# Fetching a third of the far degree factors from HBM and moving the message product to ScalarE in a three-layer graph kernel

## The chip, the cores and the metric

The kernel runs on one core of a Trainium2 chip. The metric is the device time of one execution in microseconds (us). The profile is one execution recorded by the hardware profiler. Engines are named as in the profile: PE is TensorE, PEld its weight loads, DVE VectorE, ACT ScalarE, POOL GpSimd. SP is the engine that issues most DMAs; "SPq" in a row is such an issue.

## The reference

A graph with 100,000 nodes of 64 features and 25,000 edges. Layer 0 is an attention layer; after it come three rounds ("layers" below, l = 0, 1, 2) of the code that matters here. Each round computes one mask value per edge, sums it per source node, and weighs far rows with it:

```python
for l in range(N_LAYERS):
    f1 = relu(x[row] @ nb_W[l] + nb_b[l])
    f2 = relu(x[col] @ self_W[l] + self_b[l])
    h = relu(concatenate([f1, f2], axis=1) @ att1_W[l] + att1_b[l])
    log_alpha = (h @ att2_W[l] + att2_b[l])[:, 0]
    mask = clip(sigmoid(log_alpha) * (ZETA - GAMMA) + GAMMA, 0.0, 1.0)
    rowsum = segment_sum(mask, row, num_segments=n) + 1e-06
    d_inv_sqrt = clip(rowsum ** (-0.5), 0.0, 10.0)
    vals = mask * d_inv_sqrt[row] * d_inv_sqrt[col]
    x = segment_sum(vals[:, None] * x[col], row, num_segments=n)
    out = out + x
```

`d_inv_sqrt[col]` is the degree factor of the edge's other end, the "far" one. In the program `x[col]` is called `far`, and `mask * d_inv_sqrt[row]` is `VAL0`.

## The kernel before

The edges stand sorted by their own node, in 196 tiles of 128 edges, four tiles to a chunk, 49 chunks (`NC1`). Each layer l has a mask stage (five matmul steps per chunk, with gathers of far rows on POOL from l = 1 on), a short degree part (`rowsum_dve`), and then the **sum stage**, which the change edits. Every engine runs its own list of steps. `staged(n, [(lag, step), ...])` writes such a list: in iteration i it emits each step for chunk i - lag, in the order given. An engine works its list strictly in that order and stops at a semaphore wait, so a step that waits also holds everything behind it. The steps of a sum stage for chunk c are:

- **spread** (SP): a DMA that broadcasts the bf16 row numbers of the chunk's far factors, `row_d`, over 128 partitions into `RB` (names `XC<-row_of_far_degree` in the trace). `RB` has two buffers.
- **hot** (ACT): two operations, Square into `OFF` and Relu into `OH`, that make a one-hot matrix of 128 x 512.
- **bring** (PE): 12 matmuls of the one-hot matrix with the table `TAB` of degree factors (three bf16 parts); two sets of banks.
- **select** (DVE): four operations that pick one column each into `DCc`, then a small product with `VAL0` into `VAL1` (signal `o_val`), and then the **product** of the far rows with `VAL1` into `Z`, 128 x 256 (signal `z_done`).
- **turn_z** (PE): two transposes of `Z`. **scan** (DVE): the segment sum over the turned rows. **turn_back** (PE): two transposes of the sums.
- In layers 0 and 1: **rows** (ACT) copies the turned sums from PSUM into `TS` (signal `q_out`), and **store** (SP) waits for `q_out` and writes them to HBM. When all are stored, POOL gathers the far rows of the next layer.
- In layer 2: **load** (SP) brings base rows and the sums of both earlier layers, three DMAs; for chunk c it waits until **final** (DVE, three additions, signal `q2_fin`) is through with chunk c - 3, whose buffer it takes. POOL then scatters the final rows to `out`, four indirect DMAs per chunk.

The lags before are: SP spread 0, store 5 (layer 2: load 2); ACT hot 0, rows 4; PE bring 0, turn_z 2, turn_back 3; DVE select 0, scan 2, final 3. So SP's order is spread(i), store(i-5), spread(i+1), and ACT's is hot(i), rows(i-4), hot(i+1). On POOL a memset of the far rows of layer 0 follows each product.

## Time and profile before

| | |
|---|---|
| median of 3 runs | 3198.88 us (3198.11 to 3206.03) |
| the profiled execution, its own time | 3199.13 us |
| span of its trace | 3197.3 us |
| sum stage of layer 0, about | 2003 to 2164 us |
| sum stage of layer 1, about | 2456 to 2618 us |
| sum stage of layer 2, to the end | 2912 to 3197 us |
| busy over the span | DVE 69%, POOL 60%, PE 56%, ACT 33% |
| mean granted clock of PE | 0.687 of full speed |

The times inside the trace count from the start of its span. A row of the timeline gives start, duration, engine, line, operation, and in brackets how long the engine had been idle and what ended that. Line numbers are those of the kernel before. Two operations in a row on DVE or ACT overlap by about a tenth of a microsecond, so the distance from start to start is shorter than the duration.

### The profile page before, as it was taken

To read this page: it belongs to the slowest core of one execution; us is meant where nothing else is said; L and a number is where in the kernel's file an instruction comes from. 1 tells how busy PE (TensorE), PEld (TensorE's weight loads), DVE (VectorE), ACT (ScalarE), POOL (GpSimd) and SP (SyncE) were. 2 spreads that over 40 slices of the span, in tenths; PEclk is the share of its full clock that TensorE was granted. 3 is DMA by queue.
4 is the path that set the end of the run, shared out by engine and by line. 5 is a ranking of instruction groups with operands and counts; after the bars stand their busy time and mean duration, and the time that the engine had idled before them with its cause. 6 is when DMAs were issued, how large, how long until landed. Compare 5 with 4: busy or idle time off the path is not lost.

```text
span 3197.3 us, 34323 instructions
## 1 busy us (share of the span) xinstructions
PE 1780.0 (56%) x8972; PEld 1443.3 (45%) x8972; DVE 2195.2 (69%) x5951; ACT 1068.3 (33%) x2292; POOL 1913.7 (60%) x1844
## 2 busy tenths in 40 slices
PE   1124444441399986653665654665665656655663
PEld 0023333331299975542454433453444544544442
DVE  6748888887877744434555553897866988766775
ACT  0024444442144420001333323553444644443221
POOL 0057777777888017776777775017773017773776
PEclk9975555565555555556777776897888987787555
DMA  0023332231122212214222211233332333333543
GB/s 7 3 54 82 84 88 82 83 86 41 41 86 86 83 60 69 71 50 96 62 63 61 64 40 34 70 85 96 98 104 64 88 88 94 102 98 84 126 119 85
DMA packets 283933, 238.03 MB, mean 74 GB/s; under 512 B 161125, under 2 KB 207611, under 8 KB 283637
## 3 DMA queue, kind: packets, MB, share of 16 engines
q1 hardware_dynamic: 226933, 196.13, 21.4%
q0 software_dynamic: 56832, 40.05, 5.5%
q8 instruction: 58, 0.95, 0.1%
q14 instruction: 110, 0.90, 0.1%
HBM read 163.62 MB, written 84.20 MB: 78 GB/s over the span
## 4 chain that ended last, share of the span: by engine, by line
POOL 48%; issue 18%; DVE 13%; PE 12%; DVEq 4%; DMA 2%; SPq 1%; ACT 1%; POOLq 0%; ACTq 0%
POOL big L1003 13%; POOL G L994 12%; POOL regs L1845 7%; POOL out L1010 6%; POOL regs L1854 5%; PE bank L923 5%; POOL x_after_layer L647 5%; DVE den L1271 3%; PE bank L916 3%; DVE big L1285 2%; DVE big L1591 2%; PE bank L872 1%; DVEq L1590 1%; PE bank L1451 1%; DVEq L1273 1%
## 5 line engine op out<-in xcount | busy, mean ns | idle before, releaser
L1003 POOL DMA_INDIRECT big<-layer_rows,late x392 | 425.9, 1087 | 305.8 <-SPq L1075 186.9
L1845 POOL DMA_INDIRECT regs<-in_x,G x200 | 213.8, 1069 | 234.8 <-DVEq L1711 174.1
L1451 PE MATMUL bank<-regs,SQ 99*128 99x256 bf16 x1764 | 274.8, 319 | 84.2 <-ACT SQ L1357 77.7
L647 POOL DMA_INDIRECT x_after_layer<-G,idx_s x200 | 197.0, 985 | 198.0 <-DVEq L808 135.9
L1870 POOL DMA_INDIRECT farf<-dst_float,VAL x196 | 252.8, 1290 | 59.7 <-issue 59.7
L1451 PEld LDWEIGHTS bank<-regs,SQ 99*128 99x128 bf16 x1764 | 189.3, 112 | 152.8 <-ACT SQ L1357 102.7
L1010 POOL DMA_INDIRECT out<-G,scat_i x196 | 194.7, 993 | 104.4 <-issue 61.4
L1854 POOL DMA_INDIRECT regs<-in_x,G x200 | 211.2, 1056 | 70.2 <-issue 59.7
L1271 DVE SCALAR_TENSOR_TENSOR den<-steps,late,bank 128x256 f32<-128x256 f32 x588 | 245.2, 472 | 9.6 <-PE bank L1451 9.3
L994 POOL DMA_INDIRECT G<-x_after_layer,own_i x196 | 200.6, 1023 | 69.2 <-issue 61.0
L994 POOL DMA_INDIRECT G<-x_after_layer,far_i x196 | 198.5, 1013 | 66.5 <-issue 66.5
L505 PE MATMUL bank<-regs 128*128 128x196 bf16 x800 | 161.2, 356 | 90.8 <-ACT regs L492 90.8
L1355 ACT ACTIVATE SQ<-XC,row_of 128x512 bf16<-128x512 bf16 x147 | 105.9, 721 | 259.4 <-DMA XC<-row_of_far_degree 235.6
L1402 PE MATMUL bank<-ident,big 128*128 128x128 f32 x196 | 50.3, 347 | 226.8 <-DMA big<-layer_rows,late 226.8
L1398 PE MATMUL bank<-ident,XC 128*128 128x128 f32 x196 | 50.3, 408 | 215.2 <-DVEq L1114 215.2
L564 ACT ACTIVATE SQ<-XC 128x512 f32<-128x512 f32 x99 | 62.3, 629 | 284.8 <-DVE XC L547 284.7
L395 DVE RECIPROCAL dstat<-dstat 128x8 f32<-128x8 f32 (+1 forms) x196 | 38.9, 198 | 169.8 <-ACT dstat L408 169.8
L885 PE MATMUL bank<-ident,VS 128*128 128x128 f32 x100 | 32.6, 426 | 212.5 <-DVE VS L717 212.5
L933 PE MATMUL bank<-big,den 128*128 (+1 forms) x400 | 95.8, 420 | 93.4 <-DVE den L587 86.5
L1402 PEld LDWEIGHTS bank<-ident,big 128*128 128x128 f32 x196 | 23.2, 166 | 271.1 <-issue 270.9
L933 PEld LDWEIGHTS bank<-big,den 128*128 128x128 f32 x400 | 87.3, 322 | 106.7 <-issue 99.4
L1398 PEld LDWEIGHTS bank<-ident,XC 128*128 128x128 f32 x196 | 33.0, 206 | 226.0 <-issue 226.0
(416 smaller groups left out, 5745.7 us busy)
## 6 DMA issues: line engine op xcount, KB each, us to landing
regs<-x_after_layer SPq DMA_DIRECT2D x96, 256.0 KB, 3.2
out<-regs SPq DMA_DIRECT2D x96, 256.0 KB, 2.1
XC<-row_of_far_degree SPq DMA_DIRECT2D x147, 128.0 KB, 3.4
den<-in_x SPq DMA_DIRECT2D x50, 256.0 KB, 2.7
x_after_layer<-den SPq DMA_DIRECT2D x50, 256.0 KB, 2.0
regs<-tile_nodes SPq DMA_DIRECT2D x50, 256.0 KB, 3.2
layer_rows<-TS SPq DMA_DIRECT2D x98, 128.0 KB, 2.0
regs<-in_x SPq DMA_DIRECT2D x46, 256.0 KB, 2.8
```

What stands on the lines that cost most here:

```text
L505: pe.matmul(o_, GE[b][h][:, k * P:(k + 1) * P], LT[:, h, part, :], start=(h + part == 0), stop=False)
L647: g.indirect_dma_start(x1_d, bass.IndirectOffsetOnAxis(ap=idx_s[:, b, k:k + 1], axis=0), G[:, b, k, 0, :], None, bounds_check=top, oob_is_ ...
L923: ins = pe.matmul(bank[4 + b][:, k * F:(k + 1) * F], ZTs[b][:, q * 512 + k * P:q * 512 + (k + 1) * P], wm[:, q, :], start=(q == 0), stop=( ...
L933: ins = pe.matmul(bank[b][:, k * F:(k + 1) * F], STg[b][:, k, :], big1[:, one(c, k), :].rearrange("p o f -> p (o f)"), start=True, stop=True)
L994: g.indirect_dma_start(G[:, b, grp // 2, grp % 2, :], None, x1_d, bass.IndirectOffsetOnAxis(ap=ix[:, u:u + 1], axis=0), bounds_check=top, ...
L1003: ahead(g, l, REVERSED, lambda u, l=l: g.indirect_dma_start(far[:, tile_of(u // C, u % C), :], None, xt_d[l - 1], bass.IndirectOffsetOnAxi ...
L1010: g.indirect_dma_start(out, bass.IndirectOffsetOnAxis(ap=scat_i[1][:, u:u + 1], axis=0), SUM[b][:, k, :], None, bounds_check=top, oob_is_e ...
L1271: v.scalar_tensor_tensor(PICK[k], steps[:, :], far_c[:, u:u + 1], bank[2 + 2 * b + k // 2][:, (k % 2) * 256:(k % 2) * 256 + 256], ALU.is_e ...
L1451: ins = pe.matmul(bank[2 + 2 * b + k // 2][:, (k % 2) * 256:(k % 2) * 256 + 256], OH[b][0:RB1 + 1, k * P:(k + 1) * P], TAB[0:RB1 + 1, part ...
L1845: g.indirect_dma_start(GR[:, c % DEEP, k, 0, :], None, a["x"], bass.IndirectOffsetOnAxis(ap=own0[:, c * C + k:c * C + k + 1], axis=0), bou ...
L1854: g.indirect_dma_start(GR[:, c % DEEP, k, 1, :], None, a["x"], bass.IndirectOffsetOnAxis(ap=far0[:, c * C + k:c * C + k + 1], axis=0), bou ...
L1870: g.indirect_dma_start(farf[:, u:u + 1], None, dstf_d, bass.IndirectOffsetOnAxis(ap=perm1[:, u:u + 1], axis=0), bounds_check=top, oob_is_e ...
```

## The change

Three things are done together.

1. In layers 0 and 1 the chunks 5, 8, 11, ..., 47 (15 of 49) are `FETCHED`: SP writes the degree factors as a table to HBM once per layer (`table_out`), and POOL gathers each fetched chunk's 512 factors from it with four indirect DMAs (`fetch_degrees`). These chunks have no spread, no hot, no bring and no picks. The other 34 are `LOOKED` and are numbered through by `g`, which picks their buffers. Layer 2 has all 49 looked up as before.
2. In all three layers the product moves from DVE to ACT, as four operations of 128 x 64 with a scale of one value per partition. It stands in ACT's list at lag 1, between hot and rows.
3. The lags behind it grow by one: scan 3, turn_back 4, rows 5, final 4. The lags of SP's list stay: store 5, load 2.

```diff
+FETCHED = [[c for c in range(NC1) if l < 2 and c >= 5 and c % 3 == 2] for l in range(3)]
+LOOKED = [[c for c in range(NC1) if c not in FETCHED[l]] for l in range(3)]
+LOOKED_BEFORE = [sum(len(LOOKED[k]) for k in range(l)) for l in range(4)]
...
+            def fetch_degrees(l):
+                g.wait_ge(signal("tables_out"), 16 + 32 * (l + 1))
+                for c in FETCHED[l]:
+                    i = fetch_index(l, c)
+                    landed = signal(f"pair{i % FARS}")
+                    if i >= FARS:
+                        g.wait_ge(landed, fetch_need(i - FARS))
+                    for u in range(C * c, C * c + C):
+                        g.indirect_dma_start(DCc[:, u:u + 1], None, deg_d, bass.IndirectOffsetOnAxis(ap=pos_i[:, u:u + 1], axis=0),
+                                             bounds_check=places, oob_is_err=False).then_inc(landed, 16)
...
+                def table_out(l=l):
+                    sp.wait_ge(signal("r_val"), l + 1)
+                    for h in range(2):
+                        sp.dma_start(at(deg_d, 256 * h, [[512, 49], [1, 256]]), DEGR[49 * h:49 * h + 49, :]).then_inc(signal("tables_out"), 16)
...
-                    staged(NC1, [(0, spread), (5, store)])
+                    staged(NC1, [(0, spread), (1, lambda c: table_out() if c == 0 else None), (5, store)])
...
             def select(c):
                 b = c % 2
...
+                if c in FETCHED[l]:
+                    i = fetch_index(l, c)
+                    v.wait_ge(signal(f"pair{i % FARS}"), fetch_need(i))
+                else:
...
                 v.tensor_tensor(VAL1[:, C * c:C * c + C], DCc[:, C * c:C * c + C], VAL0[:, C * c:C * c + C], ALU.mult).then_inc(signal("o_val"), 1)
-                if c >= 2:
-                    v.wait_ge(signal("z_t"), l * NC1 + c - 1)
-                v.drain()
-                v.tensor_tensor(by_pair(Z[b]), by_pair(far[:, C * c:C * c + C, :]), bc(VAL1[:, C * c:C * c + C].rearrange("p (h q) -> p q h", h=2), F), ALU.mult).then_inc(signal("z_done"), 1)
...
-            staged(NC1, [(0, select), (2, scan)] + ([(3, final)] if l == 2 else []))
+            staged(NC1, [(0, select), (3, scan)] + ([(4, final)] if l == 2 else []))
...
-                staged(NC1, [(0, hot)] + ([(4, rows)] if l < 2 else []))
+
+                def product(c, l=l):
+                    b = c % 2
+                    s_.wait_ge(signal("o_val"), l * NC1 + c + 1)
+                    if c >= 2:
+                        s_.wait_ge(signal("z_t"), l * NC1 + c - 1)
+                    for k in range(C):
+                        u = C * c + 2 * (k % 2) + k // 2
+                        ins = s_.activation(Z[b][:, k, :], far[:, C * c + k, :], ACT.Copy, scale=VAL1[:, u:u + 1])
+                    ins.then_inc(signal("z_done"), 1)
+                staged(NC1, [(0, hot), (1, product)] + ([(5, rows)] if l < 2 else []))
...
-                staged(NC1, [(0, bring), (2, turn_z), (3, turn_back)])
+                staged(NC1, [(0, bring), (2, turn_z), (4, turn_back)])
```

On SP, in the sum stage of layer 0, the list begins like this before (`XC<-row_of_far_degree` is a spread, `layer_rows0<-TS` a store):

```order
L1058 DMA XC<-row_of_far_degree 128x512 [waits h_cc,h_t,row_out]
L1058 DMA XC<-row_of_far_degree 128x512
L1058 DMA XC<-row_of_far_degree 128x512 [waits o_hot] x4
L1062 DMA layer_rows0<-TS 128x4x64 [waits q_out]
L1058 DMA XC<-row_of_far_degree 128x512 [waits o_hot]
L1062 DMA layer_rows0<-TS 128x4x64 [waits q_out]
```

and like this after:

```order
L1093 DMA XC<-row_of_far_degree 128x512 [waits h_cc,h_t,row_out]
L1093 DMA XC<-row_of_far_degree 128x512
L1084 DMA degree_of_place<-den 49x256 [waits r_val]
L1084 DMA degree_of_place<-den 49x256
L1093 DMA XC<-row_of_far_degree 128x512 [waits o_hot] x3
L1097 DMA layer_rows0<-TS 128x4x64 [waits q_out]
L1093 DMA XC<-row_of_far_degree 128x512 [waits o_hot]
L1097 DMA layer_rows0<-TS 128x4x64 [waits q_out]
L1093 DMA XC<-row_of_far_degree 128x512 [waits o_hot]
L1097 DMA layer_rows0<-TS 128x4x64 [waits q_out] x2
```

Store(i-5) still stands between spread(i) and spread(i+1); of each three spreads one is gone, its store is not, and the table goes out behind the second spread.

On ACT, in the same stage, from the hot of chunk 5 on before (L1355 and L1357 are hot, L1348 is rows):

```order
L1355 ACTIVATE SQ<-XC,row_of 128x512 [waits o_mm,o_ids1]
L1357 ACTIVATE SQ<-SQ,one_c 128x512
L1348 ACTIVATE TS<-bank7 128x2x2x64 [waits s_bt]
L1355 ACTIVATE SQ<-XC,row_of 128x512 [waits o_mm,o_ids0]
L1357 ACTIVATE SQ<-SQ,one_c 128x512
L1348 ACTIVATE TS<-bank6 128x2x2x64 [waits q_stored0,s_bt]
```

and after, from the product of chunk 4 on (L1394 and L1396 are hot, L1405 the product, L1384 is rows; `bank6` and `bank7` take turns with the chunk, so the first rows(0) is the one with `bank6`):

```order
L1405 ACTIVATE den<-big,VAL1 128x64 [waits z_t,o_val]
L1405 ACTIVATE den<-big,VAL1 128x64 x3
L1384 ACTIVATE TS<-bank6 128x2x2x64 [waits s_bt]
L1394 ACTIVATE SQ<-XC,row_of 128x512 [waits o_mm,o_ids1]
L1396 ACTIVATE SQ<-SQ,one_c 128x512
L1405 ACTIVATE den<-big,VAL1 128x64 [waits z_t,o_val]
L1405 ACTIVATE den<-big,VAL1 128x64 x3
L1384 ACTIVATE TS<-bank7 128x2x2x64 [waits s_bt]
L1394 ACTIVATE SQ<-XC,row_of 128x512 [waits o_mm,o_ids0]
```

Before, the rows of chunk 1 (`bank7`) follow the hot of chunk 5; now they follow the hot and the product of the next iteration, that of chunks 6 and 5. The rows of chunk i-5 stood ahead of hot(i) and now stand behind it.

On DVE, where the sum stage of layer 2 comes to its first final, before (L1285 is scan, L1271 and L1274 are select, L1278 is the product, L1295 to L1301 are final; `bank4` and `bank5` belong to odd chunks, `bank2` and `bank3` to even ones):

```order
L1285 SCALAR_TENSOR_TENSOR big<-regs,bank0 128x256 [waits z_t]
L1271 SCALAR_TENSOR_TENSOR den,late<-steps,late,bank4 128x256 [waits o_mm]
L1271 SCALAR_TENSOR_TENSOR den,late<-steps,late,bank4 128x256
L1271 SCALAR_TENSOR_TENSOR den,late<-steps,late,bank5 128x256 x2
L1274 TENSOR_TENSOR VAL1<-late,VAL0 128x4
L1278 TENSOR_TENSOR den<-big,VAL1 128x256 [waits z_t]
L1285 SCALAR_TENSOR_TENSOR big<-regs,big,bank1 128x256 [waits z_t,s_scan]
L1295 TENSOR_TENSOR regs<-regs 128x256 [waits q2_ld0]
L1299 TENSOR_TENSOR G<-bank6,regs 128x256 [waits s_bt]
L1301 TENSOR_TENSOR G<-G,regs 128x256
```

and after (L1321 is scan, L1311 and L1314 are select, L1331 to L1337 are final):

```order
L1321 SCALAR_TENSOR_TENSOR big<-regs,bank0 128x256 [waits z_t]
L1311 SCALAR_TENSOR_TENSOR den,late<-steps,late,bank2 128x256 [waits o_mm]
L1311 SCALAR_TENSOR_TENSOR den,late<-steps,late,bank2 128x256
L1311 SCALAR_TENSOR_TENSOR den,late<-steps,late,bank3 128x256 x2
L1314 TENSOR_TENSOR VAL1<-late,VAL0 128x4
L1321 SCALAR_TENSOR_TENSOR big<-regs,big,bank1 128x256 [waits z_t,s_scan]
L1331 TENSOR_TENSOR regs<-regs 128x256 [waits q2_ld0]
L1335 TENSOR_TENSOR G<-bank6,regs 128x256 [waits s_bt]
L1337 TENSOR_TENSOR G<-G,regs 128x256
```

The first final, that of chunk 0, stood behind the select of chunk 3 and now stands behind that of chunk 4.

## Rows read from the trace of the kernel before

**Rows 1.** Page: span, then costly groups (busy us, mean ns, idle before)
```profile
span 3197.3 us, 34323 instructions
...
L1870 POOL DMA_INDIRECT farf<-dst_float,VAL x196 | 252.8, 1290 | 59.7 <-issue 59.7
L1010 POOL DMA_INDIRECT out<-G,scat_i x196 | 194.7, 993 | 104.4 <-issue 61.4
L1271 DVE SCALAR_TENSOR_TENSOR den<-steps,late,bank 128x256 f32<-128x256 f32 x588 | 245.2, 472 | 9.6 <-PE bank L1451 9.3
```

**Rows 2.** Windows: length, busy PE PEld DVE ACT POOL, clock, DMA share, GB/s
```profile
400.00:440.00 40.00, 17.31 (x99) 13.92 (x100) 32.82 (x119) 19.23 (x39) 30.86 (x31) 0.59 0.30 87
2003.00:2164.00 161.00, 107.41 (x788) 81.32 (x788) 146.01 (x552) 88.63 (x148) 15.25 (x49) 0.92 0.34 79
2912.00:3197.00 285.00, 162.74 (x788) 113.36 (x788) 201.59 (x697) 71.01 (x99) 194.67 (x196) 0.58 0.44 110
```

**Rows 3.** Timeline of one chunk's period in the sum stage of layer 0
```profile
2060.50 0.51 SPq L1058 DMA_DIRECT2D XC<-row_of_far_degree  x1
...
2060.80 0.16 DVE L1274 TENSOR_TENSOR VAL<-late,VAL 128x4 f32<-128x4 f32 x1
...
2061.06 0.42 DVE L1278 TENSOR_TENSOR den<-big,VAL 128x256 f32<-128x256 f32 x1
...
2061.40 0.74 DVE L1285 TENSOR_TENSOR_SCAN big<-regs,big,bank 128x256 f32<-128x256 bf16 x1
...
2062.51 1.48 PE L1451 MATMUL bank<-regs,SQ 99*128 99x256 bf16 x12
2062.67 0.38 ACT L1348 ACTIVATE TS<-bank 128x256 f32<-128x256 f32 x1 [0.22 <-PE bank L1476]
...
2063.08 0.37 SPq L1062 DMA_DIRECT2D layer_rows<-TS  x1
...
2063.50 0.50 SPq L1058 DMA_DIRECT2D XC<-row_of_far_degree  x1
...
2063.91 0.72 ACT L1355 ACTIVATE SQ<-XC,row_of 128x512 bf16<-128x512 bf16 x1 [0.85 <-DMA XC<-row_of_far_degree]
...
2064.70 0.72 ACT L1357 ACTIVATE SQ<-SQ,one_c 128x512 bf16<-128x512 bf16 x1
```

**Rows 4.** Page, DMA issues: count, KB each, median us to landing
```profile
XC<-row_of_far_degree SPq DMA_DIRECT2D x147, 128.0 KB, 3.4
```

**Rows 5.** Groups by form on ACT, SBUF to SBUF without a per-partition operand
```profile
L564 ACT ACTIVATE SQ<-XC 128x512 f32<-128x512 f32 x99 | 62.3, 629 | 284.8 <-DVE XC L547 284.7
...
L1318 ACT ACTIVATE big<-XC 128x256 f32<-128x256 f32 x49 | 20.5, 418 | 77.9 <-DVEq L1114 77.9
```

**Rows 6.** Timeline of ACT: fifth hot of layer 0's sum stage
```profile
2016.73 0.72 ACT L1357 ACTIVATE SQ<-SQ,one_c 128x512 bf16<-128x512 bf16 x1
```

**Rows 7.** Timeline of ACT: last hot and last rows of that stage
```profile
2151.89 0.72 ACT L1357 ACTIVATE SQ<-SQ,one_c 128x512 bf16<-128x512 bf16 x1
...
2161.65 0.38 ACT L1348 ACTIVATE TS<-bank 128x256 f32<-128x256 f32 x1 [1.43 <-PE bank L1476]
```

**Rows 8.** Timeline of the sum stage of layer 2: from final(1) to select(7)
```profile
2936.27 0.43 DVE L1301 TENSOR_TENSOR G<-G,regs 128x256 f32<-128x256 f32 x1
...
2938.12 0.59 SPq L1058 DMA_DIRECT2D XC<-row_of_far_degree  x1
...
2942.05 0.72 ACT L1355 ACTIVATE SQ<-XC,row_of 128x512 bf16<-128x512 bf16 x1 [3.29 <-DMA XC<-row_of_far_degree]
...
2943.62 2.74 PE L1451 MATMUL bank<-regs,SQ 99*128 99x256 bf16 x12 [1.21 <-ACT SQ L1357]
...
2948.17 0.16 DVE L1274 TENSOR_TENSOR VAL<-late,VAL 128x4 f32<-128x4 f32 x1
...
2949.49 0.40 DVE L1295 TENSOR_TENSOR regs<-regs 128x256 f32<-128x256 f32 x1
```

**Rows 9.** Line L1301, last operation of final: durations ns, first and last start
```profile
L1301 DVE TENSOR_TENSOR G<-G,regs x33: 424/425/427, 2932.1 to 3180.3; 128x256 f32<-128x256 f32 x33
```

More of the change, by code:

```diff
@@ L975, in ahead_done, with fetch_index, fetch_need @@
                 eng.wait_ge(signal(f"ring{k}"), ROWS_IN + (16 * C) * ((use + 1) * len(range(k, NC1, RING))))
+        def fetch_index(l, c):
+            return l * len(FETCHED[0]) + FETCHED[l].index(c)
+        def fetch_need(i):
+            return 16 * C * (len(range(i % FARS, NCH, FARS)) + i // FARS + 1)
         FORWARD, REVERSED = list(range(NC1)), list(range(NC1))[::-1]
@@ L996, in L1_pool @@
             g.wait_ge(signal("pos_split"), 1)
+            for c in FETCHED[0]:
+                g.memset(DCc[:, C * c:C * c + C], 10.0)
+            g.drain()
+            fetch_degrees(0)
             for c in range(NC1):
@@ L1004, in L1_pool @@
                     far[:, tile_of(u // C, u % C), :], None, xt_d[l - 1], bass.IndirectOffsetOnAxis(ap=pos_i[:, u:u + 1], axis=0), bounds_check=top, oob_is_err=False))
+                if l < 2:
+                    fetch_degrees(l)
             for c in range(NC1):
@@ L1053, in L1_sp @@
             for l in range(LAYERS):
+                def table_out(l=l):
+                    sp.wait_ge(signal("r_val"), l + 1)
+                    for h in range(2):
+                        sp.dma_start(at(deg_d, 256 * h, [[512, 49], [1, 256]]), DEGR[49 * h:49 * h + 49, :]).then_inc(signal("tables_out"), 16)
                 def spread(c, l=l):
-                    b = c % 2
-                    if l or c >= 2:
-                        sp.wait_ge(signal("o_hot"), l * NC1 + c - 1)
+                    if c not in LOOKED[l]:
+                        return
+                    g = LOOKED_BEFORE[l] + LOOKED[l].index(c)
+                    b = g % 2
+                    if g >= 2:
+                        sp.wait_ge(signal("o_hot"), g - 1)
                     sp.dma_start(RB[b], row_d[:, C * P * c:C * P * (c + 1)].broadcast_to([P, C * P])).then_inc(signal(f"o_ids{b}"), 16)
@@ L1249, in rowsum_dve @@
             if l:
-                v.wait_ge(signal("o_mm"), NC1 * l)
+                v.wait_ge(signal("o_mm"), LOOKED_BEFORE[l])
             v.tensor_copy(TAB[0:RB1, 0, :], DEGR)
@@ L1350, in hot @@
                 def hot(c, l=l):
-                    b = c % 2
-                    s_.wait_ge(signal(f"o_ids{b}"), half_need(b, l, c))
-                    if c >= 2:
-                        s_.wait_ge(signal("o_mm"), l * NC1 + c - 1)
+                    if c not in LOOKED[l]:
+                        return
+                    g = LOOKED_BEFORE[l] + LOOKED[l].index(c)
+                    b = g % 2
+                    s_.wait_ge(signal(f"o_ids{b}"), 16 * (g // 2 + 1))
+                    if g >= 2:
+                        s_.wait_ge(signal("o_mm"), g - 1)
                     s_.activation(OFF[b], RB[b], ACT.Square, bias=row_of[:, 0:1])
@@ L1442, in bring @@
                 def bring(c, l=l):
-                    b = c % 2
+                    if c not in LOOKED[l]:
+                        return
+                    i = LOOKED[l].index(c)
+                    g = LOOKED_BEFORE[l] + i
+                    b = g % 2
                     if c == 0:
                         pe.wait_ge(signal("r_carry"), 2 * l + 2)
-                    pe.wait_ge(signal("o_hot"), l * NC1 + c + 1)
-                    if c >= 2:
-                        pe.wait_ge(signal("o_val"), l * NC1 + c - 1)
+                    pe.wait_ge(signal("o_hot"), g + 1)
+                    if i >= 2:
+                        pe.wait_ge(signal("o_val"), l * NC1 + LOOKED[l][i - 2] + 1)
                     for k in range(C):
@@ L1819, in _ @@
             top = g.to_reg(N - 1)
+            places = g.to_reg(SL1 - 1)
             for o in range(2):
@@ L1876, in _ @@
             L0_pool(g, top)
-            L1_pool(g, top)
+            L1_pool(g, top, places)
 mid_side, end_side = [], []
```

16 lines of the change are left out of this document (9 added, 7 removed).

## The prediction

> **What bounds the kernel now.** I read the page first, then the windows of the three sum stages, then one chunk's period in the timeline, row by row, and at last the order in which SP and ACT emit their steps. The page alone misleads here: it shows ACT with a third of its time busy, and DVE as the busiest engine.
>
> In the sum stages of layers 0 and 1 DVE is the engine that never rests: 146 of 161 us [rows 2]. The spreads leave SP at 2060.50 and 2063.50, so a chunk takes 3.00 us [rows 3]. DVE spends that on the picks (245.2 us over 147 chunks, 1.67 each [rows 1]), VAL1, the product (0.34 from its start to the scan's) and the scan (0.66 to the next picks). Both stages have 49 chunks and the same picture.
>
> There is a second loop, nearly as long, that the page doesn't name. A spread left at 2063.50 only because the store ahead of it on SP waited for rows, which ACT began at 2062.67 [rows 3]. From its issue to the hot that uses it go 3.41 us (2060.50 to 2063.91), the usual landing time [rows 3, 4]. ACT idled 0.85 us for it. Before the change rows(i-5) is emitted ahead of hot(i), so the spread of i+1 is issued before hot(i) starts, and the landing is covered by a whole chunk. The loop is: spread, 3.41 landing, hot 1.42 to ACT's next operation, rows 0.38, store 0.42, and that serves two chunks: 5.66 / 2 = 2.8 us, just under DVE's 3.00.
>
> The sum stage of layer 2 is paced by POOL's scatters: four of 0.99 us with 0.31 of issue between them, 5.2 us a chunk [rows 1]. The last operation of final starts first at 2932.1 and last at 3180.3, 48 chunks later: 5.17 us each [rows 9].
>
> **The change, part by part.**
>
> DVE loses the product everywhere, 0.34 us a chunk, and the picks of 15 chunks, 1.67 us each: 49 x 0.34 + 15 x 1.67 = 41.7 us per stage of layers 0 and 1. This is a gain only if DVE stays the bound.
>
> POOL's gathers: 60 per layer. The nearest rows are the gathers of one element per partition from `dst_float`, 1.29 us plus 0.30 of issue [rows 1]; a fetched chunk costs POOL 6.4 us. POOL has nothing else in these stages but the memsets (15.25 us [rows 2]). At one fetched chunk in three, due every 9 us or later, they are hidden; the lower bound is 1.0 us a gather, and both ends are hidden. The table costs two small DMAs on SP, behind the second spread: hidden too.
>
> The product on ACT: no row has a 128 x 64 form. From 256 to 512 columns an operation grows from 0.418 to 0.629 [rows 5], 0.82 ns a column, so 64 columns would take 0.26; a per-partition operand adds 0.09 (0.72 for hot [rows 3] against 0.629), so 0.335. Back to back they start 0.09 earlier: 0.24 each, 0.96 for four. Bounds: 0.65 without operand, 1.7 if a small one cost as much as 256 columns.
>
> Now the lags, which decide. On SP store stays at lag 5. On ACT rows goes from 4 to 5. So **rows(i-5) now stands behind hot(i)**, and spread(i+1), which stands behind store(i-5), is issued only after hot(i) has run, which itself waited for spread(i). The two `RB` buffers are never both in use. Between two looked chunks: landing 3.41, hot 1.42, product 0.96, rows 0.38, signal 0.03, store 0.42 = **6.62 us**.
>
> Around a fetched chunk f it is longer, since no hot stands between hot(f-1) and product(f-1). From the end of hot(f-1): bring 2.74 and select to `o_val` 1.97 (2943.62 to 2948.33 is 4.71 in all [rows 8]), 0.05 ahead of it and 0.03 behind, product 0.96, rows 0.38, signal and store 0.45: 6.6 to spread(f+1), then 3.41 + 1.51 to the end of hot(f+1): **11.5 us**. Three chunks take 6.6 + 11.5 = 18.1 us where they took 9.0.
>
> PE's clock enters through bring: 1.48 us at 2.4 GHz [rows 3], 2.74 at 1.2 [rows 8]. PE would be busy about half of the time at the low level (two brings of 2.74 and six transposes of 0.64 in 18.1). Where PE was busy 43% the mean grant was 0.59, and 0.58 at 57% in layer 2; only the dense stage, 67%, had 0.92 [rows 2]. I take the low level for four fifths. The Trainium skill's page "TensorE: Matmul & The Clock Gate" (Part 1: The HAM clock gate) says the throttled state is the default and activity releases it; by that alone I would put everything at the low level, and the trace agrees that sparser work had the lower grant.
>
> Sum for one stage of layers 0 and 1, low level: hot(4) ended at 2017.45 and hot(48) at 2152.61 [rows 6, 7], 135.2 us. Now from hot(4) to hot(48): 14 x 18.1 + 11.5 = 264.9; **+130**. Ahead of that, product(2) waits for select(2) and holds hot(4): about +5 (bring 2.74, select 1.97 and 0.96 against nothing). Behind it bring and product are longer, +2. Together **+137**. At the high level each of the 15 fetched chunks costs 1.26 less, 246.0, and the ends nothing to speak of: +113.
>
> Layer 2: SP emits spread(i), load(i-2), spread(i+1). Load(i-2) waits for final(i-5). That final was in DVE's iteration i-2 and is now in i-1. So a loop from final(i-5) over spread(i+1) and select(i+1) came back at final(i-2), three chunks on; now it comes back at final(i-3), two on. Its length: from the end of final(1), 2936.70, to the end of select(7), 2948.33, are 11.63 us; scan 0.76 and final's three operations of 0.40 to 0.43, 1.25, make 13.6, with a landing of 3.9 in that row [rows 8] against the usual 3.4 [rows 4]. I take **13.3**. Before: 13.6 / 3 = 4.5, hidden under POOL's 5.2. Now 6.65 a chunk: not hidden. 22 such pairs lead from final(0) to final(44), the last with a spread behind it: 293 us; the last four go at POOL's 5.2; final(0) comes 4.2 later. 318 against 248.2: **+69**. At the high level 12.0 a pair: +41.
>
> Total: 2 x 137 + 69 = +343 at the low level, 2 x 113 + 41 = +267 at the high one; 0.8 and 0.2 of them give +328. The profiled execution took 3199.13, 1.8 over its span, and 0.25 from the median: **3527 us**.
>
> On the landing, the page "DMA: Bandwidth & Descriptors" of the Trainium skill (Anatomy of one DMA, software path) gives about 2.0 us plus bytes over 436 GB/s, 2.3 for 128 KB. By that estimate a loop would be 1.1 shorter, 80 times in all (29 in each of two stages, 22 in the third), and the sum 3439. The measured 3.4 is for this very transfer on SP's path and decides.
>
> **Rivals.**
> - *Only the loops of layers 0 and 1*: layer 2 hides its own under POOL, if finals come early enough in pairs. Then +226 to +274, 3425 to 3473. Against it: 13.3 for two exceeds POOL's 10.3 by 3 us, while ACT already waited 3.29 for the spread [rows 8]. 8%.
> - *The stores don't hold the spreads*; ACT's order does. Hot(f-1), 4.8 to `o_val`, product, rows, hot(f+1), then one more hot, product, rows: 7.6 + 2.7 = 10.3 per three chunks (9.0 at the high level). That is 0 to 19 us a stage, with 7 at the ends, and 41 to 69 in layer 2: 3254 to 3320, about 3290. Against it: the spread at 2063.50 came right behind the store at 2063.08 [rows 3]. 3%.
> - *Faster*: DVE stays the bound and gives its 41.7 us twice: 3199 - 83 = 3116. It needs ids landed well ahead, that is a spread issued 3.41 + 1.51 + 1.48 = 6.4 us or more before its picks, more than two periods; with one spread in flight at a time this fails as soon as landing, hot, product, rows and store exceed a period. They sum to 6.6. 3%.
> - *Next to nothing*: losses and gains cancel, 3199. 2%.
>
> The forecast has 84%.
>
> **How the numbers follow.** A landing of 4.0 instead of 3.4 adds 80 x 0.6 = 48 us (3575); all at the high level is 3466; without layer 2's loop 3425 at the least. The range is 3430 to 3590 and leaves some 10% out. A measurement of this kernel tells 0.3%, 10 us, from no change. Slower: 84 + 8 + 3 = 95%; faster 3%, the same 2%.
>
> **What would show it.** In the sum stages of layers 0 and 1: each spread issued behind a store, after the hot of the looked chunk before; distances of 6.6 and 11.5 us between the ends of hots; DVE busy well under half; about 298 us a stage instead of 161; ACT's long waits put down to the DMA. POOL's gathers over after about 100 us. In layer 2: finals in pairs, 13.3 us from pair to pair, POOL idle about a fifth of the time. It would be wrong if a spread were issued while the one before is still unused, if bring ran at the high level throughout, or if four products took far from 1 us.

## The result, and the profile after

| | before | after |
|---|---|---|
| median | 3198.49 us (4 runs, 3192.61 to 3206.03) | 3542.81 us (4 runs, 3539.18 to 3549.38) |
| the profiled execution, its own time | 3199.13 us | 3539.18 us |
| span of its trace | 3197.3 us | 3537.4 us |
| mean granted clock of PE | 0.687 | 0.635 |

The changed kernel takes 1.107 times as long (95% interval 1.106 to 1.109): 344 us more. Executions of one kernel fall into a faster and a slower state, and every ratio in this document compares the fast ones alone, so it can differ from the quotient of the medians. DVE is busy 102 us less (2195.2 before), ACT 96 and POOL 120 more (1068.3 and 1913.7 before), and neither of these two is near its limit; what grew most is idle time. These are the page's span, its busy times and its costly groups (busy us, mean ns of one, then idle time before them and what ended it):

```profile
span 3537.4 us, 33733 instructions
...
PE 1843.9 (52%) x8612; PEld 1473.6 (42%) x8612; DVE 2093.2 (59%) x5564; ACT 1164.0 (33%) x2820; POOL 2033.4 (57%) x1979
...
L1311 DVE SCALAR_TENSOR_TENSOR den<-steps,late,bank 128x256 f32<-128x256 f32 x468 | 197.1, 476 | 505.9 <-PE bank L1504 505.8
...
L1394 ACT ACTIVATE SQ<-XC,row_of 128x512 bf16<-128x512 bf16 x117 | 84.2, 719 | 388.1 <-DMA XC<-row_of_far_degree 388.1
...
L1405 ACT ACTIVATE den<-big,VAL 128x64 f32<-128x64 f32 x588 | 155.0, 334 | 163.5 <-DVE VAL L1314 163.4
L1005 POOL DMA_INDIRECT late<-degree_of_place,late x120 | 119.5, 996 | 91.7 <-DMA degree_of_place<-den 55.7
...
XC<-row_of_far_degree SPq DMA_DIRECT2D x117, 128.0 KB, 3.4
```

The picks (L1311) fell from 245.2 us busy to 197.1, and the idle time before them rose from 9.6 us to 505.9 [rows 1]. Read on from there: the picks wait for bring (L1504), bring for hot, and hot (L1394) waits 388.1 us in all for the spread to land, where the page of before has 235.6 us for it, and more hots (147 instead of 117). Yet landing takes what it took, 3.4 us [rows 4]. So the transfers didn't become slower; they are issued later. This is hot's line on the page of before:

```profile
L1355 ACT ACTIVATE SQ<-XC,row_of 128x512 bf16<-128x512 bf16 x147 | 105.9, 721 | 259.4 <-DMA XC<-row_of_far_degree 235.6
```

The windows of the three sum stages place the loss (columns as in [rows 2]):

```profile
2003.00:2301.00 298.00, 136.56 (x608) 95.28 (x608) 104.24 (x382) 110.41 (x313) 74.25 (x109) 0.53 0.16 37
2590.00:2891.00 301.00, 137.07 (x608) 95.59 (x608) 105.30 (x384) 111.00 (x313) 59.76 (x60) 0.54 0.16 35
3190.00:3537.00 347.00, 162.11 (x788) 114.19 (x788) 181.41 (x647) 119.31 (x294) 193.69 (x196) 0.60 0.36 90
```

Against 161 us, 162 and 285 before [rows 2] that is 137, 139 and 62 more, 338 of the 340 us by which the span grew. DVE is busy for 35% of layer 0's stage, where it was 91%. Three chunks take 18.21 us (median over layer 0, from the ends of hots) and 18.34 (layer 1), against 9.0 and 9.1 before.

One period of layer 0 in the timeline of ACT, a fetched chunk in it (start, duration, what it is, idle time before it and what ended that):

```profile
2249.94 0.72 ACT L1394 ACTIVATE SQ<-XC,row_of 128x512 bf16<-128x512 bf16 x1 [3.73 <-DMA XC<-row_of_far_degree]
...
2256.54 0.72 ACT L1394 ACTIVATE SQ<-XC,row_of 128x512 bf16<-128x512 bf16 x1 [3.86 <-DMA XC<-row_of_far_degree]
...
2257.96 1.05 ACT L1405 ACTIVATE den<-big,VAL 128x64 f32<-128x64 f32 x4
2258.91 0.36 ACT L1384 ACTIVATE TS<-bank 128x256 f32<-128x256 f32 x1
2262.85 1.06 ACT L1405 ACTIVATE den<-big,VAL 128x64 f32<-128x64 f32 x4 [3.58 <-DVE VAL L1314]
2263.82 0.36 ACT L1384 ACTIVATE TS<-bank 128x256 f32<-128x256 f32 x1
2268.29 0.72 ACT L1394 ACTIVATE SQ<-XC,row_of 128x512 bf16<-128x512 bf16 x1 [4.11 <-DMA XC<-row_of_far_degree]
```

and in that of SP (an "x2" row spans two issues, with the wait of the second between them):

```profile
2252.70 0.36 SPq L1097 DMA_DIRECT2D layer_rows<-TS  x1
2253.11 0.50 SPq L1093 DMA_DIRECT2D XC<-row_of_far_degree  x1
2259.30 5.27 SPq L1097 DMA_DIRECT2D layer_rows<-TS  x2
2264.61 0.50 SPq L1093 DMA_DIRECT2D XC<-row_of_far_degree  x1
```

and, between hot and the second product, on PE (bring) and on DVE (`VAL1`, behind the picks):

```profile
2258.11 2.74 PE L1504 MATMUL bank<-regs,SQ 99*128 99x256 bf16 x12 [3.00 <-ACT SQ L1396]
...
2262.66 0.16 DVE L1314 TENSOR_TENSOR VAL<-late,VAL 128x4 f32<-128x4 f32 x1
```

Follow one spread. It leaves at 2253.11; hot starts 3.43 us later, at 2256.54; product 1.42 after that, rows 0.95 after the product; rows begins at 2258.91, and 0.39 later the store leaves. Where the next chunk is looked up, its spread stands right behind this store, as the one of 2253.11 stood behind the store of 2252.70. One looked chunk takes 2256.54 - 2249.94 = 6.60 us. Here the next chunk is the fetched one, which has neither spread nor hot. The product that comes next on ACT is that of the hot of 2256.54. It needs bring and the picks of this hot, and so begins only at 2262.85, 4.80 us after the end of hot (2258.05); ACT idles for 3.58 of them. The second store leaves near 2264.2, the spread at 2264.61, the hot at 2268.29. That is 11.75 us. In neither step is there more than one spread in flight.

In layer 2 the timeline of DVE shows the finals (last operation, L1337) in pairs, where they came every 5.17 us on average before [rows 9]:

```profile
3295.26 0.42 DVE L1337 TENSOR_TENSOR G<-G,regs 128x256 f32<-128x256 f32 x1
...
3304.57 0.43 DVE L1337 TENSOR_TENSOR G<-G 128x256 f32<-128x256 f32 x1
...
3308.42 0.43 DVE L1337 TENSOR_TENSOR G<-G,regs 128x256 f32<-128x256 f32 x1
...
3317.80 0.42 DVE L1337 TENSOR_TENSOR G<-G,regs 128x256 f32<-128x256 f32 x1
```

Their distances are 9.3, 3.9 and 9.4 us. From the first final to the last are 306.8 us (3213.5 to 3520.4 in the view of line L1337), against 248.2 [rows 9]. The timeline of all engines, between the finals at 3304.57 and 3317.80:

```profile
3305.02 0.33 SPq L1103 DMA_DIRECT2D G<-base_rows  x1
...
3306.43 0.50 SPq L1093 DMA_DIRECT2D XC<-row_of_far_degree  x1
...
3310.11 0.72 ACT L1394 ACTIVATE SQ<-XC,row_of 128x512 bf16<-128x512 bf16 x1 [5.86 <-DMA XC<-row_of_far_degree]
...
3311.68 2.74 PE L1504 MATMUL bank<-regs,SQ 99*128 99x256 bf16 x12 [5.79 <-ACT SQ L1396]
...
3318.50 0.98 POOL L1037 DMA_INDIRECT out<-G,scat_i  x1 [3.20 <-DVE G L1337]
```

The final lets the load go (3305.02, right at the end of the final), behind the load stands the spread (3306.43), and 11.8 us after that the first final of the next pair is through (3317.80 and 0.42). POOL's scatter waited 3.20 us for it.

### The profile page after: what moved, and what is told of

Same layout as the page of the kernel before. It is cut to its first block, busy times and chain, and to the rows that moved or that the text cites. A ratio compares the mean times of both kernels' runs of the same rounds, so it can differ in the third digit from the quotient of the medians.

```text
span 3537.4 us, 33733 instructions
## 1 busy us (share of the span) xinstructions
PE 1843.9 (52%) x8612; PEld 1473.6 (42%) x8612; DVE 2093.2 (59%) x5564; ACT 1164.0 (33%) x2820; POOL 2033.4 (57%) x1979
## 4 chain that ended last, share of the span: by engine, by line
POOL 39%; issue 15%; PE 14%; DVE 11%; DMA 10%; ACT 6%; DVEq 3%; SPq 3%; ACTq 0%; POOLq 0%
POOL big L1028 12%; POOL G L1015 11%; DMA XC<-row_of_far_degree 8%; POOL regs L1899 6%; POOL regs L1908 5%; PE bank L1504 5%; POOL x_after_layer L651 4%; PE bank L927 4%; DVE den L1311 3%; PE bank L920 2%; ACT SQ L1394 2%; ACT den L1405 2%; DVE big L1644 1%; PE bank L876 1%; ACT SQ L1396 1%
## 5 line engine op out<-in xcount | busy, mean ns | idle before, releaser
L1504 PE MATMUL bank<-regs,SQ 99*128 99x256 bf16 x1404 | 304.3, 403 | 397.5 <-ACT SQ L1396 392.9
L1311 DVE SCALAR_TENSOR_TENSOR den<-steps,late,bank 128x256 f32<-128x256 f32 x468 | 197.1, 476 | 505.9 <-PE bank L1504 505.8
L1504 PEld LDWEIGHTS bank<-regs,SQ 99*128 99x128 bf16 x1404 | 186.3, 140 | 504.6 <-ACT SQ L1396 432.3
L651 POOL DMA_INDIRECT x_after_layer<-G,idx_s x200 | 197.1, 986 | 193.3 <-DVEq L812 131.2
L1394 ACT ACTIVATE SQ<-XC,row_of 128x512 bf16<-128x512 bf16 x117 | 84.2, 719 | 388.1 <-DMA XC<-row_of_far_degree 388.1
L1405 ACT ACTIVATE den<-big,VAL 128x64 f32<-128x64 f32 x588 | 155.0, 334 | 163.5 <-DVE VAL L1314 163.4
L1005 POOL DMA_INDIRECT late<-degree_of_place,late x120 | 119.5, 996 | 91.7 <-DMA degree_of_place<-den 55.7
```

Source lines behind the costliest of these rows:

```text
L651: g.indirect_dma_start(x1_d, bass.IndirectOffsetOnAxis(ap=idx_s[:, b, k:k + 1], axis=0), G[:, b, k, 0, :], None, bounds_check=top, oob_is_ ...
L1311: v.scalar_tensor_tensor(PICK[k], steps[:, :], far_c[:, u:u + 1], bank[2 + 2 * (g % 2) + k // 2][:, (k % 2) * 256:(k % 2) * 256 + 256], AL ...
L1394: s_.activation(OFF[b], RB[b], ACT.Square, bias=row_of[:, 0:1])
L1405: ins = s_.activation(Z[b][:, k, :], far[:, C * c + k, :], ACT.Copy, scale=VAL1[:, u:u + 1])
L1504: ins = pe.matmul(bank[2 + 2 * b + k // 2][:, (k % 2) * 256:(k % 2) * 256 + 256], OH[b][0:RB1 + 1, k * P:(k + 1) * P], TAB[0:RB1 + 1, part ...
```

## The experiments

No kernel here leaves out work: all of them change only lags, or the engine of the product. They ran on four chips. On the chip of e1b and e3b the kernel before took 3199 us, as in the result above, but on the three others, called disturbed below, it took 3936, 3892 and 3776 us. No trace of it was kept there. The same kernel on either kind of chip, e3_rows5 and e3b_rows5, shows where such time goes. Of 715 us more in the span, 374 lie ahead of the first hot of layer 0's sum stage, 156 and 133 between the hots of one sum stage and those of the next, and 54 behind the first hot of layer 2's: in all these stretches POOL issues indirect DMAs. In the sum stages of layers 0 and 1, where it issues none, there is no difference (last column of the table). In the stretches with them the other engines stand still at times, for 10 us and more (the last section shows rows).

Ratios are always to the kernel before on the same chip. On the disturbed chips single executions of one kernel lie up to 6% apart (the kernel before 3794 to 3950 us on one, e7b 3757 to 3984 on another), so totals settle little there. From those three chips I use mainly the pace of stretches in which POOL issues no indirect DMAs, and "three chunks" below is a median over a sum stage, layer 0 / layer 1:

| kernel | three chunks, us | first to last hot, us |
|---|---|---|
| before | 9.00 / 9.09 | 147.2 / 147.1 |
| after | 18.21 / 18.34 | 284.3 / 286.5 |
| e1_store6, e1b_store6 | 11.63 / 11.63, 11.54 / 11.61 | 249.2 / 248.8, 186.4 / 187.9 |
| e2_load3, e2b_load3 | 18.24 / 18.29, 18.04 / 17.97 | 347.2 / 337.8, 339.5 / 338.5 |
| e3_rows5, e3b_rows5 | 17.16 / 17.09, 17.19 / 17.15 | 260.8 / 259.5, 261.3 / 260.6 |
| e4_fetch_only, e4b, e4c | 9.38 / 9.28, 9.43 / 9.50, 9.54 / 9.71 | 217.8 / 219.5, 216.2 / 220.4, 216.3 / 217.1 |
| e5_both_lags | 11.59 / 11.59 | 247.3 / 248.2 |
| e7_deeper, e7b_deeper | 9.19 / 8.88, 9.15 / 8.99 | 210.4 / 209.0, 209.1 / 207.5 |

Where a kernel ran on both kinds of chip, the pace is the same within 0.1 us. e3, whose sum stages have no gathers on POOL, agrees in the last column too (260.8 and 261.3); the kernels that fetch have some 62 us more there on a disturbed chip (249.2 against 186.4).

The theory: spread(i+1) stands behind store(i-5), that waits for rows(i-5), and rows(i-5) now stands behind hot(i) (**store loop**); in layer 2 spread(i+1) stands behind load(i-2), that waits for a final one iteration later than before (**load loop**). The rivals: the order on ACT by itself, or the gathers and the product as work.

**e1_store6 and e1b_store6: SP gives back the iteration that ACT took.**

```diff
-                    staged(NC1, [(0, spread), (1, lambda c: table_out() if c == 0 else None), (5, store)])
+                    staged(NC1, [(0, spread), (1, lambda c: table_out() if c == 0 else None), (6, store)])
```

> The changed kernel with store at lag 6 instead of 5 in SP's list (layers 0 and 1), nothing else. Theory (the spread of the next chunk is held by a store whose rows stand behind the current hot): spreads go out one hot earlier, the two sum stages fall from 298 us to 180 to 200 each, layer 2 stays at its 13 us pairs; total 3300 to 3345. Rival (the added work itself costs: four products on ACT, the gathers of single factors on POOL, contention of their DMAs): 3530 to 3550, the stages stay near 298.

Measured on the first disturbed chip: 4153.68 us, ratio 1.055 (1.050 to 1.059) to 3935.99. That total can't be set against the changed kernel's, which was not measured on that chip. The same kernel on the chip where the one before takes 3199 us:

> The same kernel as e1_store6 (store at lag 6 in SP's list of layers 0 and 1), again on a chip where the kernel before takes its usual 3199 us. Theory (the next spread is held by a store whose rows stand behind the current hot): the two sum stages fall from 298 us to 180 to 200 each, total 3300 to 3345. Rival (the added work costs): 3530 to 3550.

Measured: 3344.97 us (3337.30 to 3348.81), ratio 1.044 (1.042 to 1.047) to 3199.38. One number in SP's list takes back 198 of 344 us, all of it in the first two sum stages (table below). They came to 200.8 and 202.3 us, just above the 180 to 200 that were expected, and the total lies at the upper edge of its range. Their waits say what is left. This is the view of waits for layer 0's stage in the changed kernel (engine, tile and line <- what ended the wait: us in all, times, longest):

```profile
ACT SQ L1394 <- DMA XC<-row_of_far_degree: 114.8, 29, 4.8
ACT den L1405 <- DVE VAL L1314: 65.3, 18, 6.6
```

and for the same stage in e1b_store6:

```profile
ACT den L1405 <- DVE VAL L1314: 61.0, 32, 6.6
...
ACT SQ L1394 <- DMA XC<-row_of_far_degree: 20.2, 20, 1.8
```

In the kernel before, hot waited 37.9 us for the landing in this stage, in the changed one 114.8, in e1b 20.2; the product's wait for `VAL1` stayed. It is the next loop, to be read from e1b's timeline of ACT:

```profile
2100.17 0.72 ACT L1394 ACTIVATE SQ<-XC,row_of 128x512 bf16<-128x512 bf16 x1 [1.13 <-DMA XC<-row_of_far_degree]
...
2106.47 1.06 ACT L1405 ACTIVATE den<-big,VAL 128x64 f32<-128x64 f32 x4 [2.17 <-DVE VAL L1314]
2107.44 0.36 ACT L1384 ACTIVATE TS<-bank 128x256 f32<-128x256 f32 x1
...
2111.59 0.72 ACT L1394 ACTIVATE SQ<-XC,row_of 128x512 bf16<-128x512 bf16 x1 [0.50 <-DMA XC<-row_of_far_degree]
```

and SP's between the last two:

```profile
2108.23 0.51 SPq L1093 DMA_DIRECT2D XC<-row_of_far_degree  x1
```

From the hot at 2100.17: 6.30 us to its own product (hot, bring, picks), 0.97 to rows, 0.79 to the spread that waited for that rows' store, 3.36 to the next hot but one: 11.42 us, and this serves three chunks, one of them fetched. So the stores still hold the spreads: this spread waited for the product of the chunk three before its own. In the changed kernel it waited for the hot or the product of the looked chunk just before. E1 doesn't open the loop; it lets it come back later, and so serve more chunks.

**e3_rows5 and e3b_rows5: the kernel before, with rows one iteration later, and nothing else.**

```diff
-                staged(NC1, [(0, hot)] + ([(4, rows)] if l < 2 else []))
+                staged(NC1, [(0, hot)] + ([(5, rows)] if l < 2 else []))
```

> The kernel before with one number changed: rows at lag 5 instead of 4 in ACT's list. No fetch, product on DVE, all other lags as before. Theory: the store loop alone makes 3.41 + 1.42 + 0.38 + 0.45 = 5.7 us a chunk from chunk 5 on instead of 3.0, 44 x 2.7 = 117 us a stage, total 3420 to 3440. Rival (the lag costs nothing, the added work does): 3190 to 3210.

Measured on the disturbed chip of e1_store6: 4122.8 us (4030.07 to 4143.31); three chunks 17.16. The same kernel on the chip of e1b:

> The same kernel as e3_rows5 (the kernel before with rows at lag 5 instead of 4 on ACT, one number), again. Theory: the store loop alone makes 5.7 us a chunk instead of 3.0 from chunk 5 on, 117 us a stage, total 3420 to 3440. Rival (the lag costs nothing): 3190 to 3210.

Measured: 3422.03 us (3418.16 to 3428.05), ratio 1.069 (1.066 to 1.072). There is no gather and no product on ACT in this kernel, and DVE, PE and POOL do the work of before. The timeline of ACT:

```profile
2109.79 0.72 ACT L1355 ACTIVATE SQ<-XC,row_of 128x512 bf16<-128x512 bf16 x1 [3.94 <-DMA XC<-row_of_far_degree]
...
2111.21 0.36 ACT L1348 ACTIVATE TS<-bank 128x256 f32<-128x256 f32 x1
```

and of SP, around it:

```profile
2106.29 0.51 SPq L1058 DMA_DIRECT2D XC<-row_of_far_degree  x1
2111.60 0.37 SPq L1062 DMA_DIRECT2D layer_rows<-TS  x1
2112.01 0.51 SPq L1058 DMA_DIRECT2D XC<-row_of_far_degree  x1
```

3.50 landing + 1.42 hot + 0.39 + 0.41 = 5.72 us a chunk, the bare store loop. The same four steps were there before the change and served two chunks (5.66 / 2 under DVE's 3.00); one lag made them serve one. That settles the store loop as cause, from both sides. E3b makes it serve one chunk in a kernel without gathers and without a product on ACT, and loses 223 us. E1b moves nothing but the stores, with ACT's order, the gathers and the product as in the change, and gains 198. What is left in e1b over the kernel before, 146 us, is 63 in layer 2 and 83 in the other two sum stages.

The length of each sum stage, from the start of the reciprocal of the degree part to the point where the next stage may read the stored rows (in layer 2 to the end of the span), us:

| | before | after | e1b_store6 | e3b_rows5 |
|---|---|---|---|---|
| layer 0 | 160.0 | 298.7 | 200.8 | 274.8 |
| layer 1 | 160.2 | 300.8 | 202.3 | 274.1 |
| layer 2 | 284.3 | 347.6 | 347.9 | 284.8 |

Layer 2 is as after in e1b and as before in e3b: its 63 us have a cause of their own, which is in neither edit.

**e2_load3 and e2b_load3: in layer 2 the loads one iteration later.**

```diff
-                    staged(NC1, [(0, spread), (2, load)])
+                    staged(NC1, [(0, spread), (3, load)])
```

> The changed kernel with load at lag 3 instead of 2 in SP's list of layer 2, nothing else. Theory (load waits for a final that now comes one iteration later and holds the next spread): layer 2's sum stage falls by 55 to 65 us back to POOL's 5.2 us a chunk, layers 0 and 1 unchanged; total 3475 to 3490. Rival (the product on ACT or the lower clock of PE lengthens layer 2): no change, 3535 to 3550.

> The same kernel as e2_load3 (the changed kernel with load at lag 3 instead of 2 in SP's list of layer 2), again. Theory (load waits for a final that now comes one iteration later and holds the next spread): layer 2's sum stage falls by 55 to 65 us to POOL's 5.2 us a chunk, layers 0 and 1 unchanged; total 3475 to 3490. Rival (the product on ACT or PE's lower clock lengthens layer 2): 3535 to 3550.

Both fell on disturbed chips: 4294.79 us (4174.61 to 4328.83; kernel before 3935.99), and 4243.90, ratio 1.099 (1.072 to 1.126). The finals are the thing to look at. The timeline of DVE in e2b_load3:

```profile
3966.18 0.43 DVE L1337 TENSOR_TENSOR G<-G,regs 128x256 f32<-128x256 f32 x1
...
3969.90 0.43 DVE L1337 TENSOR_TENSOR G<-G 128x256 f32<-128x256 f32 x1
...
3974.42 0.43 DVE L1337 TENSOR_TENSOR G<-G,regs 128x256 f32<-128x256 f32 x1
...
3983.80 0.42 DVE L1337 TENSOR_TENSOR G<-G,regs 128x256 f32<-128x256 f32 x1
```

3.7, 4.5, 9.4: threes where there were pairs, as a loop must do that comes back one chunk later. The chips don't make the threes: in e1_store6, on a disturbed chip and with the load at lag 2, the finals come in pairs as in the changed kernel. In e3_rows5 and the e4 runs, whose layer 2 has the lists of before, they come in threes there too: two distances of 4.2 us, then one or two long ones. So the grouping goes with the lag between load and final.

From the first final to the last, e2_load3 took 286.3 us, against 305.2 in e1_store6 and 302.6 in e3_rows5 on the same chip, and e2b_load3 289.3, against 306.2 in e4b_fetch_only on its chip. The load's lag is thus worth 19 us there. That is not the 58.6 us that this stretch lost on an undisturbed chip, and the finals did not come back to the expected 5.2 us a chunk: 286.3 / 48 = 6.0. In this stage, too, other engines stand still at times on these chips (DVE for 2.77 and 2.74 us in the stretch shown, where the trace names no instruction of this core that ended the wait), while POOL's four scatters of a chunk take 4.8 to 4.9 us, as on the undisturbed chip.

Of the rivals, PE's clock is out: its grant in layer 2 was 0.58 before [rows 2] and 0.60 after, and bring took 2.74 us in the rows of both. The product on ACT shows no cost of its own: with it and the load at lag 3, this stretch is shorter than with it on DVE and the lists of before, on the same chips. So the form of the loop is shown, and its size is not isolated. Of the three edits in layer 2 (product on ACT, scan and final one later) none was tried alone, and the load at lag 3 was not measured on an undisturbed chip.

**e5_both_lags: store 6 and load 3.**

```diff
-                    staged(NC1, [(0, spread), (1, lambda c: table_out() if c == 0 else None), (5, store)])
+                    staged(NC1, [(0, spread), (1, lambda c: table_out() if c == 0 else None), (6, store)])
...
-                    staged(NC1, [(0, spread), (2, load)])
+                    staged(NC1, [(0, spread), (3, load)])
```

> The changed kernel with store at lag 6 and load at lag 3, both loops opened. Theory: the savings of the two single edits add, 3345 - 58 = 3287; what is left over the kernel before, some 90 us, is the way from hot over bring and select to the product on ACT, which holds hot of two chunks on, at PE's low clock. Rival (one of the two edits only moves the wait): over 3310.

Measured on a disturbed chip: 4069.98 us, ratio 1.059 (1.041 to 1.077). Three chunks 11.59, finals 287.4 us from first to last: by pace each edit does what it does alone, and they don't touch each other. The expected total, 3287, was not put to the test. With three chunks at 11.59 against 9.0, the two together don't reach the kernel before in the first two sum stages.

**e4_fetch_only, e4b and e4c: the gathers stay, the product goes back to DVE and all lags to those of before.**

```diff
...
+                if c >= 2:
+                    v.wait_ge(signal("z_t"), l * NC1 + c - 1)
+                v.drain()
+                v.tensor_tensor(by_pair(Z[b]), by_pair(far[:, C * c:C * c + C, :]), bc(VAL1[:, C * c:C * c + C].rearrange("p (h q) -> p q h", h=2), F), ALU.mult).then_inc(signal("z_done"), 1)
...
-            staged(NC1, [(0, select), (3, scan)] + ([(4, final)] if l == 2 else []))
+            staged(NC1, [(0, select), (2, scan)] + ([(3, final)] if l == 2 else []))
...
-                def product(c, l=l):
...
-                staged(NC1, [(0, hot), (1, product)] + ([(5, rows)] if l < 2 else []))
+                staged(NC1, [(0, hot)] + ([(4, rows)] if l < 2 else []))
...
-                staged(NC1, [(0, bring), (2, turn_z), (4, turn_back)])
+                staged(NC1, [(0, bring), (2, turn_z), (3, turn_back)])
```

> The fetch of every third chunk's factors alone: product back on DVE, all lags as before. Theory (the fetch is hidden on POOL and takes picks off DVE): the store loop, one chunk ahead as before, leaves about 9.5 to 9.8 us saved per stage, total 3175 to 3190. Rival (single-factor gathers slow the kernel, by contention or late landing): 3210 or more.

> The same kernel as e4_fetch_only (only the fetch of every third chunk's factors; product on DVE, all lags as before), again. Theory (the fetch is hidden on POOL and takes picks off DVE): some 10 us saved per stage, total 3175 to 3190; if PE drops to its low clock because it has a third less to do, bring of 2.74 us takes it back, 3200 to 3240. Rival (single-factor gathers land late or slow the other DMAs): DVE waits for the gathers, 3210 or more.

> The same kernel as e4_fetch_only (the fetch alone; product on DVE, all lags as before), again on such a chip. Theory (the fetch is hidden on POOL, and what it takes off DVE is given back by PE's lower clock and the one-ahead store loop): three chunks take 9.3 us, as in the steady part of the first profiles of this kernel, total 3190 to 3215. Rival (single-factor gathers land late or slow the other DMAs): 3250 or more.

Measured, all three on disturbed chips: 4090.14 us, ratio 1.029 (1.021 to 1.037); 4082.55, 1.064 (1.053 to 1.075); 3911.52, 1.036 (1.017 to 1.055). The kernel before has no gathers in these stages and so no stalls there, so the ratios charge the fetch with the chip's disturbance. The pace doesn't: 9.3 to 9.7 us for three chunks, with a third of the picks gone, against 9.0 to 9.1 with all of them. Here is e4b's timeline of ACT, past the gathers (L1388 is rows, L1398 is hot's first operation):

```profile
2554.96 0.72 ACT L1398 ACTIVATE SQ<-XC,row_of 128x512 bf16<-128x512 bf16 x1 [0.35 <-DMA XC<-row_of_far_degree]
...
2557.38 0.38 ACT L1388 ACTIVATE TS<-bank 128x256 f32<-128x256 f32 x1 [0.90 <-PE bank L1524]
...
2561.49 0.72 ACT L1398 ACTIVATE SQ<-XC,row_of 128x512 bf16<-128x512 bf16 x1 [0.68 <-DMA XC<-row_of_far_degree]
```

and SP's:

```profile
2554.64 3.51 SPq L1097 DMA_DIRECT2D layer_rows<-TS  x2
2558.19 0.50 SPq L1093 DMA_DIRECT2D XC<-row_of_far_degree  x1
```

The spread of 2558.19 stands behind two stores, the second of which waited for the rows that ACT began at 2557.38, behind the hot of 2554.96 and behind turn_back (L1524); the hot that it feeds starts at 2561.49. So around a fetched chunk this list too issues a spread only when the one before is used up, and the step takes 2561.49 - 2554.96 = 6.5 us. Less work on DVE didn't shorten the period: the 10 us a stage that the first two expectations would save don't show. That it is this order around the missing hot which eats what DVE gives is read from the rows; no run took it away alone. PE's clock has a share that wasn't separated either: past the gathers its grant was 0.72 to 0.76 in the e4 runs, against 0.92 before [rows 2], and the turn_back that rows waited for stood behind a bring of 2.77 us. Whether the fetch alone gains a little on an undisturbed chip is open.

**e7_deeper and e7b_deeper: more room everywhere.** Store 8, load 4, product 2, rows 6, scan 4, final 5, turn_z 3, turn_back 5:

```diff
...
-                staged(NC1, [(0, hot), (1, product)] + ([(5, rows)] if l < 2 else []))
+                staged(NC1, [(0, hot), (2, product)] + ([(6, rows)] if l < 2 else []))
...
-                staged(NC1, [(0, bring), (2, turn_z), (4, turn_back)])
+                staged(NC1, [(0, bring), (3, turn_z), (5, turn_back)])
```

> The changed kernel with every step behind select one iteration later still (product 2, turn_z 3, scan 4, turn_back 5, rows 6, final 5) and store at 8, load at 4, so that neither SP's waits nor the product stand in the way of the next hot. Theory (what is left after both lags is the product's wait for select on ACT): the sum stages of layers 0 and 1 take 136 us at PE's high clock and 178 at its low one against 161 before, total 3150 to 3235, about 3200 with the clock in between. Rival (ACT has too much to do, or the gathers cost): 3270 or more.

> The same kernel as e7_deeper (every step behind select one iteration later than in the change, store at 8, load at 4), again on a chip where the kernel before takes its usual 3199 us. Theory (both of SP's loops and the product's wait are opened): three chunks take 8.9 us, as in the steady part of the first profile of this kernel, layer 2's finals come every 5.2 us on average; total 3195 to 3225. Rival (the fetch and the product on ACT cost by themselves, whatever the order): 3270 or more.

Measured on disturbed chips: 4016.91 us, ratio 1.042 (1.025 to 1.060); 3802.97, 1.014 (1.0005 to 1.028). Three chunks 8.9 to 9.2 us, that of before. Past the gathers hot no longer waits for the landing in e7b; the products wait for the buffers of `Z` instead, which turn_z frees (29.5 us in 31 waits from 2332 to 2450, in the view of waits; ACT's timeline of e7b):

```profile
2404.47 1.06 ACT L1405 ACTIVATE den<-big,VAL 128x64 f32<-128x64 f32 x4 [1.46 <-PE bank L1514]
```

From first to last hot it took 209.1 us in layer 0. Without the 62 us or so that a disturbed chip adds there to a kernel that fetches, that is 147, by estimate, and 147.2 before: no gain and no loss. The expected total, 3195 to 3225, was not put to the test. No version was shown to beat the kernel before.

## Why the prediction was right, and where a size was off

- *The store loop.* As forecast: spread, landing, hot, product, rows, store, 6.60 us measured where 6.62 was summed; e3b and e1b show it as the cause. For the loop before the change the prediction writes 5.66, where the four terms that it lists give 5.63: the 0.03 of the signal is in the sum and not in the list.
- *Around a fetched chunk* 11.75 measured for 11.5. The wait at the product was 4.80, as forecast from [rows 8]; the 0.25 more is landing, 3.68 us for 3.41. Three chunks: 18.21 and 18.34, forecast 18.1. From hot(4) to hot(48) 266.6 and 268.4 us, forecast 264.9.
- *The product on ACT.* 0.334 us each (forecast 0.335), 0.95 to 0.97 for four. The prediction's own terms, 0.26 and 0.09, give 0.35 and not 0.335, so that its number met the measured one is luck, as far as its rows go; the difference is worth 0.06 us a loop. The page "ScalarE: Activation LUTs" of the Trainium skill (What ACT_TABLE_LOAD costs) gives 186 ns, 0.833 a column and 93 for a pointer operand, 332 for this form, and says that operations back to back overlap by about 93; the trace agrees: 334 ns each, and four in 1.05 to 1.06 us where four times 334 would be 1.34.
- *The gathers.* 0.996 us each and 0.30 of issue (forecast 1.0 to 1.6): the lower end. POOL had them behind it after 82 us in layer 0, counted from 2003. Hidden, on this chip.
- *The load loop.* 13.1 us a pair (median) for 13.3; +58.6 from first to last final and +63 for the stage, for 69. The finals in pairs are in the trace; that loads one iteration later turn them into threes supports the way it was derived. That this loop is worth the whole 63 us was not shown by a run of its own.
- *The mis-sized term: PE's clock.* At the low level the sum was +137, +137, +69 = 343; measured are +138.7, +140.6, +63.3. I mixed in a fifth at the high level, which took 15 us off, and that is the distance from 3527 to 3542.81. The granted clock in the two stages was 0.53 and 0.54, that is, nearly all at 1.2 GHz, and bring took 2.74 in the period shown. The rule of the Trainium skill's page "TensorE: Matmul & The Clock Gate" that the prediction cites (the throttled state is the default), and by which it would have put everything at the low level, would have given the better number. That the sum at the low level meets the total within 1 us is in part luck: it is 2 and 4 us short in layers 0 and 1 and 6 too long in layer 2.
- *The rivals.* "Only the loops of layers 0 and 1" is out: layer 2 lost 63 us. "The stores don't hold the spreads" is out by e1b, where the stores' lag alone gave back 198 us; "faster" is out because DVE was busy for 35% of the stage, and "next to nothing" by the total. The prediction treated DVE's 41.7 us a stage as a gain if the spreads were ahead. The pace of e4, without any gain, shows that it was not within reach with the lags of before either.

## What to carry to other kernels

In a list that an engine works in order, a lag is a promise to the other lists: when a step moves one iteration later on one engine (rows on ACT), find every step on other engines that waits for it (store), and look at what stands behind that one (the next spread), for a prefetch in that place turns into a round trip. Write the loop out and count how many chunks it serves; here four unchanged steps of 5.7 us served two chunks, under DVE's 3.0 each, and then one. And an engine's busy share says nothing of what unloading it will bring while a second loop lies 0.2 us under it, as in this kernel.
